# Graph network kernel, opening stage: edge rows loaded as overlapping runs from another queue, and two sets of loads moved between queues

## The reference, cut to what matters

```python
row, col = edge_index[0], edge_index[1]              # src, dst
msg_in = jnp.concatenate([x[row], x[col]], axis=-1)
messages = jax.nn.relu(msg_in @ W_msg + b_msg)
aggregated = jax.ops.segment_sum(messages, col, num_segments=x.shape[0])
h = jax.nn.relu(jnp.concatenate([x, aggregated], axis=-1) @ W_upd + b_upd)
```

## Time and profile before

| | us |
|---|---|
| median of 3 runs | 2780.43 |
| lowest and highest | 2780.08, 2782.35 |
| profiled execution, its own time | 2774.67 |
| its span, first to last instruction | 2772.6 |
| busy: DVE, POOL, PE, ACT | 1589.9, 1436.7, 1354.4, 674.0 |
| mean granted TensorE clock | 0.742 of full speed |

### The profile page before, as it was taken

How to read it: one execution, slowest core, us unless ns; L and a number is a source line. 1 busy time by engine, 2 the same in 40 slices (tenths; PEclk the granted TensorE clock), 3 DMA queues, 4 the chain that set the end, 5 groups by cost and what they waited for, 6 DMA issues and landing times. The chain is left out here.

```text
span 2772.6 us, 26946 instructions
## 1 busy us (share of the span) xinstructions
PE 1354.4 (49%) x7570; PEld 1068.0 (39%) x7570; DVE 1589.9 (57%) x3262; ACT 674.0 (24%) x1528; POOL 1436.7 (52%) x1444
## 2 busy tenths in 40 slices
PE   3677787888589999979990000000001411111104
PEld 2466676777389997545660000000000300000003
DVE  2467777776689998532224666666665344443342
ACT  1112222212457775111120000000002233333331
POOL 2177777776300000301016777777754377777774
PEclk9789999999789999989995555555555655555557
DMA  2487777773166663010004566666651466666664
GB/s 80 129 242 230 234 238 235 234 236 102 47 164 155 153 156 92 26 10 14 9 16 122 190 190 197 191 196 194 194 181 53 132 208 209 211 211 211 211 210 135
DMA packets 272030, 433.06 MB, mean 156 GB/s; under 512 B 108749, under 2 KB 181031, under 8 KB 271883
## 3 DMA queue, kind: packets, MB, share of 16 engines
q1 hardware_dynamic: 202635, 247.61, 27.1%
q0 software_dynamic: 66784, 183.09, 24.5%
q10 hardware_dynamic: 2464, 0.64, 0.1%
HBM read 302.15 MB, written 128.80 MB: 155 GB/s over the span
## 5 line engine op out<-in xcount | busy, mean ns | idle before, releaser
L1753 POOL DMA_INDIRECT att_rows<-att_table,lane_source x416 | 463.2, 1113 | 126.7 <-issue 126.7
L2079 POOL DMA_INDIRECT best_rows<-message_source_table,lane_source x416 | 393.5, 946 | 167.2 <-issue 126.4
L735 POOL DMA_INDIRECT msg_rows<-message_source_table,msg_index x416 | 399.6, 961 | 146.4 <-issue 126.5
L2190 DVE SCALAR_TENSOR_TENSOR best_state<-best_state,lane_line,best_ps_rows 128x256 f32<-128x256 f32 x416 | 199.8, 480 | 316.3 <-ACT best_ps_rows L2104 298.0
L1785 PE MATMUL att_ps_upto<-ident,att_largest 128*4 128x128 f32 x1 | 0.4, 375 | 608.0 <-DVE att_largest L1850 608.0
L863 PE MATMUL msg_ps_sum<-msg_by_edge,msg_rows 128*128 128x128 f32 x1664 | 229.9, 296 | 110.2 <-DVE aggT L795 108.5
L863 PEld LDWEIGHTS msg_ps_sum<-msg_by_edge,msg_rows 128*128 128x128 f32 x1664 | 215.2, 208 | 142.2 <-issue 141.1
L2104 ACT ACTIVATE best_ps_rows<-best_rows,lane_weight 128x256 f32<-128x256 f32 x416 | 173.5, 462 | 359.4 <-DMA best_rows<-message_source_table,lane_source 359.4
L2138 PE MATMUL best_ps_self<-w_selfT,hT 128*125 128x256 f32 x100 | 51.7, 671 | 398.7 <-DVE x L2196 387.4
L1785 PEld LDWEIGHTS att_ps_upto<-ident,att_largest 128*4 128x4 f32 x1 | 0.1, 82 | 608.8 <-DVE att_largest L1850 608.8
L847 PE MATMUL msg_ps_window<-msg_window,msg_by_node 128*128 128x256 f32 x832 | 211.0, 400 | 22.7 <-DMA msg_window<-message_window_table 20.0
(11 more groups left out here) (290 smaller groups left out, 2713.8 us busy)
## 6 DMA issues: line engine op xcount, KB each, us to landing
att_states<-aggT SPq DMA_DIRECT2D x104, 528.0 KB
msg_window<-message_window_table SPq DMA_DIRECT2D x416, 128.0 KB
best_states<-best_state SPq DMA_DIRECT2D x104, 512.0 KB
attr_rows<-in_edge_attr SPq DMA_DIRECT2D x103, 192.0 KB, 3.3
msg_line<-place_line SPq DMA_DIRECT2D x52, 256.0 KB, 4.8
attr_line<-mask_line SPq DMA_DIRECT2D x52, 256.0 KB, 4.0
attr_carry<-carry_line SPq DMA_DIRECT2D x52, 256.0 KB
msg_rows<-message_source_table,msg_index POOLq DMA_INDIRECT x416
```

The source lines that it names most:

```text
L735: nc.gpsimd.indirect_dma_start(rows[:, s, t, :], None, table, bass.IndirectOffsetOnAxis(ap=index[:, s, t:t + 1], axis=0)).then_inc(self.ro ...
L1753: nc.gpsimd.indirect_dma_start(rows[:, t % ring, :], None, self.attention_table, bass.IndirectOffsetOnAxis(ap=self.lane_source[:, t:t + 1] ...
L2079: nc.gpsimd.indirect_dma_start(rows[:, g % SLOTS, t, :], None, table, bass.IndirectOffsetOnAxis(ap=self.lane_source[:, g * TG + t:g * TG + ...
L2190: nc.vector.scalar_tensor_tensor(out=state[:, g % STATE_BUFS, t, :], in0=before, scalar=self.lane_line[:, n:n + 1], in1=weighed_row(n), op ...
```

## The change

The edge rows are loaded with one more element on either side: `dst_rows` is [104, 4, 130] and holds the tile with its two neighbours, each row a run of the flat array that overlaps the next by two elements. `before`, `after` and their float copies are dropped, and the comparisons read shifted views of one tile. The eight loads of `dst_rows` and `src_rows` are issued by GpSimd's queue, ahead of its weight loads, after two clears by VectorE. The lanes get a column in front in the same way (`lane_dst` [128, 417], three loads, the main one of 126 rows), which replaces `lane_last`; these three are all that ScalarE's queue issues. The two loads of `base` move to SyncE's queue behind the parts of `x`. SyncE waits for the edge lines only at block 12, not ahead of the first store. The chain has 11 steps for 17, the lanes 14 for 16, and PE turns the edges after block 12. The clearing of `aggT` is cut in three. In the message pass the loads for the update are issued by ScalarE's queue.

```diff
-        lines_made, lane_steps = 17, 16
+        lines_made, lane_steps = 11, 14
...
+            def run_of(first, rows, size):
+
+                return bass.AP(dst.tensor, dst.offset + first, [[step, n] for step, n in rows] + [[1, size]])
+            full_rows = FULL - whole
+            transfers = [
+                (dst_rows[0:1, 0, 1:P + 2], run_of(0, [(P, 1)], P + 1)),
+                (dst_rows[1:RT, 0, :], run_of(P - 1, [(P, RT - 1)], P + 2)),
+                (dst_rows[:, 1:RQ - 1, :], run_of(RT * P - 1, [(P, RT), (RT * P, RQ - 2)], P + 2)),
+                (dst_rows[0:full_rows, RQ - 1, :], run_of(whole * P - 1, [(P, full_rows)], P + 2)),
+                (dst_rows[full_rows:full_rows + 1, RQ - 1, 0:REST + 1], run_of(FULL * P - 1, [(P, 1)], REST + 1)),
...
+            lane_transfers = [
+                (lane_dst[0:1, 1:LANE + 1], run_of(0, [(LANE, 1)], LANE)),
+                (lane_dst[1:LANES_FULL, :], run_of(LANE - 1, [(LANE, LANES_FULL - 1)], LANE + 1)),
+                (lane_dst[LANES_FULL:P, 0:LANE_REST + 1],
+                 run_of(LANES_FULL * LANE - 1, [(LANE, 1)], LANE_REST + 1))]
...
-                    sp.wait_ge(chain, lines_made)
+                    for tile, flat in first_nodes:
+                        sp.dma_start(tile, flat, allow_slow_non_contiguous=True).then_inc(lines_out, 16)
                     lines = ((self.mask_line, mask), (self.place_line, rel16), (self.carry_line, carry))
-                    for line, rows in lines:
-                        sp.dma_start(line.rearrange("(q r c) -> r q c", r=RT, c=P), rows[:]).then_inc(lines_out, 16)
                     for b in range(NB):
+                        if b == edges_at:
+                            sp.wait_ge(chain, lines_made)
+                            for line, rows in lines:
+                                sp.dma_start(line.rearrange("(q r c) -> r q c", r=RT, c=P), rows[:]
+                                             ).then_inc(lines_out, 16)
                         sp.wait_ge(copied, b + 1)
...
+                    pool.wait_ge(clears, 2)
+                    for tile, flat in transfers:
+                        pool.dma_start(tile, flat, allow_slow_non_contiguous=True).then_inc(loads, 16)
                     for half in range(2):
...
-                    nc.gpsimd.memset(self.aggT[:], 0.0)
+                    for k in range(3):
+                        nc.gpsimd.memset(self.aggT[:, k, :], 0.0)
...
-                    act.wait_ge(clears, 4)
-                    for tile, flat in transfers:
-                        act.dma_start(tile, flat, allow_slow_non_contiguous=True).then_inc(loads, 16)
                     act.wait_ge(lane_clears, 2)
...
-                    link(nc.vector.tensor_copy(before_f[:], before[:]))
-                    link(nc.vector.tensor_copy(after_f[:], after[:]))
...
-                    link(nc.vector.tensor_copy(other[:, :, 0:P - 1], dst_f[:, :, 1:P]))
-                    link(nc.vector.tensor_copy(other[:, :, P - 1:P], after_f[:].unsqueeze(2)))
-                    link(nc.vector.tensor_tensor(flag[:], dst_f[:], other[:], ALU.not_equal))
+                    own = dst_f[:, :, 1:P + 1]
+                    link(nc.vector.tensor_tensor(rel[:], own, dst_f[:, :, 1:2].to_broadcast([RT, RQ, P]), ALU.subtract))
+                    link(nc.vector.tensor_tensor(flag[:], own, dst_f[:, :, 2:P + 2], ALU.not_equal))
...
-                    link(nc.vector.tensor_copy(other[:, :, 1:P], dst_f[:, :, 0:P - 1]))
-                    link(nc.vector.tensor_copy(other[:, :, 0:1], before_f[:].unsqueeze(2)))
-                    link(nc.vector.tensor_tensor(flag[:], dst_f[:], other[:], ALU.not_equal))
+                    link(nc.vector.tensor_tensor(flag[:], own, dst_f[:, :, 0:P], ALU.not_equal))
...
-                    if ahead:
-                        self.load(sp, *ahead)
                     pipelined(sp, [(fetch_index, 3), (fetch_window, 0)])
...
+                    if ahead:
+                        self.load(act, *ahead)
```

## The result

The median went from 2780.26 us (2778.51 to 2782.35, 4 runs) to 2747.24 us (2744.80 to 2748.91, 4 runs), on the same chip: a ratio of 0.988, 95% interval 0.9863 to 0.9897, or 33.0 us less. The forecast was 2741.5, and 2747.24 lies in its range of 2733 to 2758.

The account below looks back on a forecast made before the run. The first gather, at 132.90 us, was taken to bound the kernel through the opening ahead of it. Gains of 25.4 (start), 8.0 (stores) and 5.5 (index) sum to 38.9 us, taking 2780.43 to 2741.5; range 2733 to 2758.

Parts of the forecast that it names:

- the root before 16 us: Sign in the opening: ScalarE's square root, which began after 40.6 us before, would come before 16 us.
- the index within 4 us: Sign at the message pass's start: the first list of source indices would land within 4 us.
- Part 1: ScalarE's queue in the opening: 18 issues removed, the three left end between 4 and 13 us, costed at nothing.
- Part 2: GpSimd's queue in the opening: eight added issues cost 4.8 us; weights, bias and aggT's clearing (to 18.4) follow, hidden.
- Part 3: VectorE's start: x's part 1 there at 17.4, hT's first copy at 20.3 instead of 45.66, gain 25.4 us.
- Rival B: Lane rows stay on one engine that x needs: part 1 at 26.2, gain 30.1, 2750 us; chance 0.14.
- Rival A: Transfers bind, not issues: edges land with x's last part at 33.7, total gain 22.3, 2758 us; chance 0.13.
- Rival C: Overlapping edge runs are cut into elements on GpSimd's queue, making the kernel slower, 2829 us; chance 0.05.
- no change: Case where the edges land just about 56 us, so the kernel's time stays as it was; chance 0.04.
- Part 4: Body of 25 blocks: eight linked VectorE steps removed give nothing, since PE sets the pace of a block.
- Part 5: Stores at the opening's end: SyncE goes on 3.9 us after the last copy instead of 11.85, gain 8.0 us.
- Part 6: Update loads on ScalarE's queue: SyncE going on to first gather takes 3.5 us instead of 9.0, gain 5.5 us.

Follow-up runs that it names:

- r11: The changed kernel once more, unchanged, on another chip: 2743.52 us against 2774.07 for the kernel before, ratio 0.9891.
- r3: The changed kernel with aggT cleared by VectorE instead of GpSimd: 2962.17 us against 2994.45 for the kernel before, on a slower chip.
- r4: The changed kernel with each part of x loaded in two transfers, 120 and 5 rows, instead of one of 125: 2963.94 us against 2994.45 for the kernel before.
- r6: The changed kernel with lanes loaded as 127 rows of 416 plus a column of 126 single elements: 2748.08 us against 2778.47 for the kernel before.
- r5: The changed kernel with the eight edge loads issued by ScalarE's queue, ahead of its lane loads: 2759.77 us against 2778.47 for the kernel before.
- r8: The kernel before, with only SyncE's stores made early and the edge lines written at block 18: 2773.87 us against 2778.47 unedited.
- r9: The changed kernel with the last three window stores issued by ScalarE and awaited by SyncE: 2740.08 us, one run, against 2774.07 for the kernel before.
- r2: The changed kernel with SyncE, not GpSimd, waiting for the window stores: 2960.86 us against 2994.45 for the kernel before.
- r10: The changed kernel with x split 120+5, weights, bias and last three window stores on ScalarE, aggT cleared by VectorE in 25 pieces: 2741.98 us, ratio 0.988.
- r1: The changed kernel with the four update loads issued by SyncE again, ahead of the first index list: 2963.62 us against 2994.45 for the kernel before.
- r12: The changed kernel with x split 120+5, aggT cleared by VectorE, last three window stores on ScalarE: 2952.64 us against 2992.9 for the kernel before, ratio 0.9877.
- r7: The changed kernel with SyncE taking the last wait, aggT cleared by VectorE and x split 120+5: 2745.65 us, ratio 0.9883 to the kernel before.

## Why the prediction was right, and where it was off

The forecast's mechanism was the right one for what was removed, and it missed what would hold the end next. Its sum was 5.0 us too large: 38.9 predicted, 33.9 found.

| step | predicted | found | off |
|---|---|---|---|
| hT's first copy | 20.3 | 22.33 | +2.0 |
| from there to the last copy's end | 66.3 | 64.6 | -1.7 |
| to SyncE going on | 3.9 | 6.95 | +3.0 |
| to the first gather | 3.5 | 5.10 | +1.6 |

The second row is luck: the same kernel in r11 has 66.2 us there, and its first gather at 100.37 makes the sum 6.4 us too large. The median stays inside the range because the range had room for misses of this size, not because these were foreseen. Of the signs given ahead, the root before 16 us (18.03) and the index within 4 us (5.10) didn't show; SyncE's wait at the end under 4 us (2.4) and the gathers of 525 us did.

**Part 1** (ScalarE's queue) was right: three issues end at 3.75, below the lower bound of 4, and ScalarE waits for VectorE. **Part 2** was right in its price (5.1 us of edge issues for 4.8) but not in taking the "clearing of aggT" to 18.4 for free. The end was right (17.97); that a step of VectorE is held up beside the clear was not seen. It was hidden all the same, as r3 shows, because x came later. Rows of before couldn't show it: there the clear ended at 12.3, ahead of any such step.

**Part 3**: x's part 1 is at 19.47 for 17.4, and that is the whole miss of this term. From 4 to 12 us the DMA engines were filled to 0.74 and 0.77:

```profile
4.00:8.00 4.00, 0.00 (x0) 0.00 (x0) 0.00 (x0) 1.06 (x1) 4.00 (x7) 1.00 0.74 200
8.00:12.00 4.00, 0.00 (x0) 0.00 (x0) 0.00 (x0) 0.00 (x0) 4.00 (x5) 1.00 0.77 206
```

The sum spread 1.42 MB evenly over the engines; that x's five carried more than their share would explain 2 us, and isn't shown. The direction is, by r4 and r6: take load off these five engines and part 0 comes at 6.66, put the lanes on one of them and part 1 comes at 26.99. **Rival B** was thus a true price (7.5 us for 8.8) of a condition that didn't hold. The Trainium skill's rule for it (DMA: Bandwidth & Descriptors, "Why a DMA increments its semaphore by 16 and not by 1"), that the number of engines is the largest up to 16 that divides the rows, agrees with r4 (120 rows for 125) and r6 (127 for 126), as far as these two edits show it.

**Rival A** is refused. The edges landed before they were wanted, and the rule that the prediction set behind it (the same page, "Issuing engines are not separate DMA queues": issuing from several engines saves only issue time, usually small) is not borne out in size: the same eight transfers cost 23.8 us of ScalarE's time in r5 and 5.1 of GpSimd's, and the first gather 17.1 us. Nor was issue time all that the move saved, since in r5 VectorE waited another 5.34 us for the edges to land. **Rival C** and no change are refused by 5.1 us for all eight issues.

**Part 4** (the body gains nothing) holds. The row it rests on is this one of before, in the waits of the engines; the row that stands in the earlier trace rows is GpSimd's wait for the same additions, and isn't the one meant. The row of after stands below it:

```profile
DVE msg_out L458 <- PE msg_table_ps_w L411: 27.3, 21, 3.3
```
```profile
DVE msg_out L462 <- PE msg_table_ps_w L416: 25.9, 21, 3.3
```

VectorE waits for PE 21 times as before. The 1.7 us less of the blocks go with the smaller shortfall of the clock (3.4 us for 5.1, table in r6).

**Part 5** failed in a step it didn't take: "SyncE goes on after 3.9". SyncE was ready after 2.9 us [its DRAIN at 89.9], better than predicted. GpSimd was costed up to the landing of its last store and no further; its DRAIN of 2.4 us lay under SyncE's burst before, grew to 3.09 with the eight DMAs more, and stands alone now. The prediction asked what a removed cover would cost elsewhere, and not here. r8 shows it at work on the kernel before, and r9 shows that with it out of the way SyncE's stores are next. So this stretch takes between 5.7 us (r2, r10) and 7.6 (r1) in every kernel with early stores, whichever of the two ends last. The first nodes took SyncE 9.7 us of issue for the 4.55 predicted, with the first store at 34.53; that was caught up, as predicted.

**Part 6**: the index took 5.10 us for 3.5. It runs beside the same update loads, and r1 shows that the order is worth 3.9 us, not 5.5. Over the runs with the index first on its queue, the time from its issue to the first gather is between 4.6 us (r12) and 7.6 (r10); what makes it differ stays open.

Behind the first gather a little is lost: the last gather is 34.2 us earlier, the attention layer's first 30.6, the last layer's first 29.4 (in two profiled executions). No line shows a new wait there, and the medians keep 33.0, so I take it as scatter of one execution.

## What to carry to other kernels

Look at which engine does the issuing before counting bytes: with loads of 103 or 127 rows ahead ScalarE was held for 7 to 12 us by one issue (7.72 in r5, 12.36 in r6), while GpSimd was free again after 0.6 us each, and here a load with one row fewer, or 120 + 5 for 125, came in sooner. When a stall at the end of a stage is removed, list what every engine does up to the meeting point, GpSimd's DRAIN among it, and take the second latest as the new end. Two covers over each other (here a clear beside a step, and a late load behind it) can show nothing when taken away one at a time; try them together.

## What the runs showed of the hardware that was not expected

- **GpSimd's DRAIN at the end of a block grows with the number of DMAs that it issued in it**: 29 DMAs 2437 ns (before, r5, r8), 31 DMAs 2600 (r10), 34 DMAs 2845 (r9, r12), 37 DMAs 3090 (after, r1, r3, r4, r6, r11), which is 82 ns for each. Where its own DMAs are still under way it lasts until after they have landed (4846 ns in r2, 5049 in r7, each 1.3 us past the point where SyncE saw them landed).
- **A clear of GpSimd holds up some of VectorE's instructions and not others.** The step from norm_mv to norm_sd, 0.17 us alone, took 3.37 and in r4 9.27 us, each time to the end of the clear, while the statistics beside the same clear kept their 1.73 us. The Trainium skill says so (SBUF — State Buffer, "Who interferes with whom"): the two engines share a port pair as an exclusive lock, and `tensor_scalar` is among those of VectorE's operations that can want it; the traces agree. In r4 the step's row begins 0.9 us before the clear's, while GpSimd issues DMAs, so which of the two held it first isn't told apart. r3, r5, r7, r10 and r12, in which no clear runs on GpSimd beside it, have 0.17 us.
- **Where rows have few divisors, a hardware queue's issue blocks**: 15.47 us for five loads of `dst_rows`, two of them of 103 rows (r5), where GpSimd's queue took 3.17; 13.63 for three lane loads of which one has 127 rows (r6) and 1.20 where it has 126 (after).
- **The 25 blocks take 61.5 to 66.3 us with the same instructions on PE**, in the order of the granted clock's shortfall (table in r6). This spread of 4.8 us is as large as the whole error of the forecast's sum.
